# Twenty products of the identity's quarters on TensorE ahead of the first projection of a decoder layer

## What is computed

```python
x = _layernorm(x + _attn(x, x, x, sa_wq, ..., True), ln1_g, ln1_b)
x = _layernorm(x + _attn(x, encoder_output, encoder_output, ca_wq, ..., False), ln2_g, ln2_b)
x = _layernorm(x + _moe(x, router_w, router_b, e_w1, e_b1, e_w2, e_b2), ln3_g, ln3_b)
```

## Time and profile before

| | |
|---|---|
| median of 3 runs | 1040.5 us (1038.59 to 1041.3) |
| profiled execution, its own time | 1039.41 us |
| span of it, first to last instruction | 1037.7 us |
| TensorE busy | 977.9 us (94%) |
| DVE, ScalarE busy | 566.6 us, 585.7 us |
| GpSimd busy | 351.7 us |
| mean granted TensorE clock | 0.981 of 2.4 GHz |

### The profile page before, as it was taken

The page is one execution under the profiler, slowest core; times in us unless marked ns, Lnnn a source line. Parts: engine busy times, 40 slices in busy tenths (PEclk is TensorE's granted clock), DMA queues, the critical chain, the costliest instruction groups (busy, mean ns, idle before and its releaser), DMA issues.

```text
span 1037.7 us, 18756 instructions
## 1 busy us (share of the span) xinstructions
PE 977.9 (94%) x6068; PEld 583.6 (56%) x6069; DVE 566.6 (55%) x949; ACT 585.7 (56%) x1201; POOL 351.7 (34%) x481
## 2 busy tenths in 40 slices
PE   5899999999999999999998999988978999999975
PEld 3446444343445543445533354226977999999964
DVE  3646587777767777776777777804221221112127
ACT  2364556777765677765666757865323343443452
POOL 8465962343144443214445042122131111111114
PEclk9999999999999999999999999989998999999988
DMA  7623452003024012108114030022030343333143
GB/s 213 165 79 102 107 135 82 23 19 105 2 69 116 22 42 55 40 1 259 39 48 123 2 92 1 6 83 67 18 108 29 112 132 116 111 106 125 37 127 126
DMA packets 71936, 84.22 MB, mean 81 GB/s; under 512 B 10688, under 2 KB 65472, under 8 KB 71744
## 3 DMA queue, kind: packets, MB, share of 16 engines
q1 hardware_dynamic: 66368, 66.06, 22.2%
q0 software_dynamic: 5504, 17.34, 5.0%
HBM read 38.89 MB, written 12.63 MB: 50 GB/s over the span
## 4 chain that ended last, share of the span: by engine, by line
PE 86%; DMA 3%; SPq 3%; ACT 2%; issue 2%; DVE 2%; POOL 1%; another core or an unknown queue 1%; DVEq 0%; ACTq 0%; POOLq 0%
PE o_bank L798 16%; PE a_bank L781 15%; PE v_slot L1242 11%; PE v_slot L754 11%; PE a_bank L1234 9%; PE a_bank L722 6%; PE a_bank L737 3%; PE o_bank L1234 3%; PE v_slot L758 3%; PE v_slot L820 2%; SPq L498 2%; PE v_slot L806 1%; PE a_bank L702 1%; PE v_slot L759 1%
## 5 line engine op out<-in xcount | busy, mean ns | idle before, releaser
L969 DVE TENSOR_REDUCE max_q<-v_slot 128x1 f32<-128x1024 f32 (+3 forms) x352 | 399.6, 1172 | 115.0 <-PE v_slot L754 72.3
L912 ACT ACTIVATE probs<-a_bank 128x512 f32<-128x512 f32 (+1 forms) x688 | 364.2, 588 | 127.8 <-PE a_bank L781 115.9
L781 PE MATMUL a_bank<-q_stack_cross,k_stack_cross 99*128 99x512 bf16 x512 | 166.0, 386 | 7.3 <-issue 5.4
L1248 ACT ACTIVATE hidden<-a_bank,b 128x128 f32<-128x128 f32 x216 | 79.1, 368 | 163.6 <-PE a_bank L1234 141.5
L754 PE MATMUL v_slot<-k_stack_cross,q_stack_cross 96*128 96x512 bf16 x512 | 148.8, 383 | 2.5 <-DMA k_stack_cross<-parts 2.4
L798 PE MATMUL o_bank<-probs,v_cross 128*32 128x512 f32 x1024 | 133.3, 607 | 0.1
L1242 PE MATMUL v_slot<-stack_or_weights,hidden 128*128 128x256 f32 x576 | 131.0, 381 | 1.1 <-DVEq L1078 1.1
L1234 PE MATMUL a_bank<-x_col,stack_or_weights 128*128 128x128 f32 x864 | 112.6, 282 | 7.2 <-ACT hidden L1248 3.7
L1242 PEld LDWEIGHTS v_slot<-stack_or_weights,hidden 128*128 128x128 f32 x576 | 107.1, 191 | 14.7 <-DVEq L1078 1.3
L1234 PEld LDWEIGHTS a_bank<-x_col,stack_or_weights 128*128 128x128 f32 x864 | 108.5, 198 | 9.7 <-issue 4.1
L781 PEld LDWEIGHTS a_bank<-q_stack_cross,k_stack_cross 99*128 99x128 bf16 x512 | 44.9, 98 | 118.5 <-ACT probs L912 68.8
(11 more groups left out here) (210 smaller groups left out, 1162.0 us busy)
## 6 DMA issues: line engine op xcount, KB each, us to landing
stack_or_weights<-in_e_w SPq DMA_DIRECT2D x16, 1024.0 KB, 6.5
stack_or_weights<-parts SPq DMA_DIRECT2D x96, 128.0 KB, 2.4
k_stack_cross<-parts SPq DMA_DIRECT2D x96, 128.0 KB, 2.5
q_stack_cross<-parts SPq DMA_DIRECT2D x48, 128.0 KB, 2.4
inputs<-in_ctxT POOLq DMA_DIRECT2D x4, 1024.0 KB, 6.7
y_got<-token_out SPq DMA_DIRECT2D x16, 256.0 KB, 6.1
x_slots<-slots_in SPq DMA_DIRECT2D x30, 129.0 KB
inputs<-in_xT POOLq DMA_DIRECT2D x4, 512.0 KB, 6.0
```

The lines of the kernel that those rows point to most:

```text
L781: last = nc.tensor.matmul(bank[:, i * cols:(i + 1) * cols], lhs, q_stack[kind][0:KM, G * u + j, q0:S], start=True, stop=True)
L912: nc.scalar.activation(probs[tile % PB][:, js[0]:js[-1] + 1, q0:S], a_bank[at % AS][:, 0:len(js) * (S - q0)].rearrange("p (j t) -> p j t", ...
L969: nc.vector.tensor_reduce(most, rows, X, ALU.max, negate=True).then_inc(v_free, 1)
L1248: nc.scalar.activation(hidden[:, f, :], h_bank[f % HB][:, 0:P], ACT.Gelu, bias=b1[:, bass.ds(e * FC + f, 1)]).then_inc(flow.gelu_done, 1)
```

## The change

TensorE gets a prologue, `warm_up`. It waits until the identity is made and then forms products of a quarter of it (32 of its rows as the stationary operand, the same 32 rows repeated four times as 512 moving columns) in float32. Quarter g uses the partitions 32g to 32g+31, writes the bank g of `a_bank[0]`, `a_bank[1]`, `a_bank[2]`, `o_bank`, and nothing reads it: the first real product into each bank starts it anew. There are seven rounds with 4, 4, 2, 2, 2, 3 and 3 products. TensorE waits at the end of each until its last product is done, and the first `split` comes behind the seventh.

```diff
@@ -302,6 +302,7 @@
         passed = sem("passed")
+        products_done = sem("products_done")
@@ -681,7 +682,26 @@
+        def warm_up(pe):
+
+            pe.wait_ge(const_made, 8)
+
+            def quarter(g, bank):
+                rows = slice(32 * g, 32 * g + 32)
+                moving = ident[rows, :].rearrange("p (o c) -> p o c", o=1).to_broadcast([32, 4, P])
+                return nc.tensor.matmul(bank[:, 0:4 * P].rearrange("p (o c) -> p o c", o=4), ident[rows, :], moving, start=True, stop=True)
+
+            banks = [a_bank[0], a_bank[1], a_bank[2], o_bank]
+            rounds = 0
+            for tiles in (4, 4, 2, 2, 2, 3, 3):
+                for g in range(tiles):
+                    last = quarter(g, banks[g])
+                last.then_inc(products_done, 1)
+                rounds += 1
+                pe.wait_ge(products_done, rounds)
+
         def attention_tensor(pe):
+            warm_up(pe)
             pe.wait_ge(first_in, 32)
```

## The result

The changed kernel takes 1056.28 us (median of 4 runs, 1048.38 to 1060.82) against 1040.76 us (4 runs, 1038.59 to 1041.3): a ratio of 1.0146, 95% interval 1.0117 to 1.0175, slower by 1.5%. Timed again in the study, it took 1050.85 us against 1039.0 us, a ratio of 1.0125 (1.0103 to 1.0147). The forecast was slower by 5.0 us; the two measurements, as differences of medians, are 15.5 and 11.9 us. A ratio is worked out from all runs of its group, so that it can lie up to 0.2% beside the quotient of two medians. One run of the kernel before and one of `one_round` took over 1430 us (1434.62 and 1437.36 us), at a mean granted clock of 0.652 and 0.650, and no median or ratio here has them.

What follows compares the result with a forecast made beforehand. SyncE's issuing behind ScalarE's first copy was taken as the bound up to 42 us; a prologue ending at 15.86 us moves that copy from 12.83 to 17.82 us, so 1040.5 + 5.0 = 1045.5 us, range 1041.5 to 1051.8 us.

Steps and rivals of the forecast that it cites:

- What bounds the start: Up to 42 us SyncE's issuing, 24 transfers in 15.56 us, starts behind ScalarE's first copy without slack.
- the cover of the prologue: TensorE's idle time from 5.41 us until the first split at 9.04 us, 3.63 us in which the prologue costs nothing.
- The ceiling of the gain: ScalarE's first copy moves at best from 12.83 to 12.16 us, held by the biases: 0.67 us.
- The round's price: A prologue round of two, three or four products costs 2.14 us at 1.2 GHz or 1.16 us at 2.4 GHz.
- the rival without sharing: In the prologue, quarters do not share the array: shift +10.7 us, 1051.2 us, or +16 us, 1056.7 us; chance 0.09.
- I take 5.1 us: TensorE's clock rises after 5.1 us of prologue, 2.4 rounds, with 3.2 and 6.8 us as bounds.
- all steps behind it move along: Everything behind ScalarE's first copy shifts by the same +5.0 us, the scores from 42.2 to 47.2 us.
- the forecast's case: Products side by side, clock up in the prologue: first copy at 17.82 us, shift +5.0 us; chance 0.62.
- the clock does not rise in the prologue: Seven rounds and the first split run at 1.2 GHz: shift +11.4 us, 1051.9 us; chance 0.13.
- The range: For the whole kernel's time, the range holding 8 in 10: 1041.5 to 1051.8 us.

Runs made afterwards that it cites:

- one_round: The change cut to its first round of four quarter products; 1038.52 us, ratio 0.9993 to the kernel before.
- two_streamed: In place of the change's rounds, two products of the whole identity without any wait; 1039.38 us, ratio 1.0002 to the kernel before.
- full_rows: The change with one product of the whole identity (128 rows) in each of seven waited rounds; 1046.9 us, ratio 1.0084 to the kernel before.
- fours: The change with four quarter products in each of its seven waited rounds; 1050.39 us, ratio 1.0103 to the kernel before.
- same_no_pause: The change's own 20 products in the same order, with only one wait at the end; 1037.47 us, ratio 1.0070 to the kernel before.
- idle_delay: The kernel before without products, TensorE waiting for GpSimd to write a block of constants a second time; 1049.38 us, ratio 1.0116.
- twos_no_pause: The change with seven groups of two quarter products, waiting only behind the last; 1048.33 us, ratio 1.0097 to the kernel before.
- rows_96_stream: The change with seven one-piece products of 96 identity rows, without waits between them; 1034.04 us (one run).
- rows_96: The change with one one-piece product of 96 identity rows in each of seven waited rounds; 1052.73 us (one run).
- threes: The change with three quarter products in each of its seven waited rounds; 1054.93 us, ratio 1.0158 to the kernel before.
- rows_64: The change with one one-piece product of 64 identity rows in each of seven waited rounds; 1050.41 us (one run).
- the change, again: The unaltered change profiled and timed a second time; 1050.85 us, ratio 1.0125 to the kernel before.

## Why the prediction was wrong

Its sign was right and its size was not: 5.0 us forecast, 15.5 and 11.9 us measured, outside of the range.

- **What bounds the start** was right. The whole shift of the first copy, 11.51 us, arrives at the first scores (11.50 us); SyncE's 24 issues take 15.74 us as against 15.56 us. The one profile of before had `xt` land late, so that the cover of the prologue usually ends up to 1 us earlier than the 9.04 us I took.
- **The ceiling of the gain** was right in kind: it gave 0.67 us, and no time was won by `two_streamed`. The ceiling itself moves with the landings: in that profile the biases held ScalarE only until 10.83 us, not 12.16 us.
- **The round's price** was right: 2.14 us at half clock forecast, 2.18 and 2.14 us measured, 1.16 us at full clock against 1.18 us (`full_rows`) and 1.23 us (`fours`). Rounds of two, three and four take 2.14, 2.16 and 2.18 us, so the quarters share the array, and the rival without sharing is out. A round of four takes 1.02 of a round with one product of the whole identity, 2.18 against 2.13 us.
- **The step that failed** is "I take 5.1 us" for the rise of the clock. The 5.1 us came from an unbroken stream of full 128-row products, and I applied it to rounds with pauses, five of them with half or three quarters of the rows. With full rows it was nearly right: `fours` rose 6.0 us behind its first product and had its first copy at 18.60 us, against my 17.82 us. The change's rounds did not raise it at all: seven rounds ran at half clock where I had counted 2.4 of them, and the first split did, too, together 11.5 us.
- **A second step was too small**: "all steps behind it move along", that is, nothing is added behind the start. `fours` is the forecast's case, with the clock up in the prologue and the first copy at +5.8 us, and it still cost 1.03% (0.72 to 1.34%), 7.5 to 13.9 us. `full_rows`, at +5.75 us, cost 0.84% (5.8 to 11.5 us), and `same_no_pause`, at +3.4 us, 0.70% (5.0 to 9.4 us). Up to 1 us of this is the late landing in the profile of before; for the rest the profiles show the wait and the stretches at 0.50 above, and the cause stays open. `idle_delay` has no such surplus: +11.35 us at the copy, 1.16% (9.9 to 14.2 us).
- **The rival** "the clock does not rise in the prologue" gave +11.4 us and 1051.9 us and is what happened, to 0.1 us at the first copy of the first profile; the repeat's 1050.85 us lies beside it, the first median's 1056.28 us 4 us above. It had 0.13. The experiments bear out both its reasons in these kernels: without the waits the change's products rose after 5.0 us (`same_no_pause`), and with all 128 rows in each round they rose after 6.0 us (`fours`). I set against them only that the first split's stream had raised the clock, which is no evidence about rounds of another kind.
- **The range** ended at 1051.8 us, just where this rival began, and had no room for a scatter of several us behind the start, which the runs of the change showed (1048.38 to 1060.82 us).

## What to carry to other kernels

Before costing work meant to raise TensorE's clock, find in the trace a stretch of the same kind, in rows of the array used and in pauses, not only in time; here streams of 128 rows rose after 5.1 to 5.5 us, which said nothing about the stream of 64 that did not rise in 12.3 us. The prologue stood ahead of the first split in TensorE's order and cost its whole length beyond its cover: it ended at 20.5 us, 11.5 us behind the cover's 9.04 us, and the first copy came 11.5 us later. So size such a prologue at the clock it starts with; and ask first what the faster start could be worth, since here the next wait left 0.67 us and nothing of it was seen in the time. The first steps are one chain here, and a delay of the start went through to the end: 11.35 us of it cost 1.16%, about 12 us. The single profile of the kernel before had a load land after 7.5 us, the thirteen others after 6.2 to 7.3 us; take such a start from more than one.

## What the hardware showed that was not expected

A TensorE that is busy in the records stayed at half clock for 12.3 us without a pause in `twos_no_pause`. At the start of these kernels, with products of 512 float32 columns, the clock rose

- after 5.1 to 5.5 us of a stream of 128 rows (before, `two_streamed`, `idle_delay`),
- after about 6 us of rounds of 128 rows with 0.4 us of pause in 2.13 us (`full_rows`, `fours`),
- after 7.0 us of a stream of 96 rows (`rows_96_stream`), and 7.0 us after the start of a round of four quarters with 0.8 us of pause and the first split behind it (`one_round`);

it did not rise in 15 us of such rounds with 96 or 64 rows (`rows_96`, `threes`, `rows_64`), nor in 12.3 us of a stream with 64 (`twos_no_pause`). Behind a prologue that had not raised it, it rose 1.7 us (the change, again) to 5.2 us (`twos_no_pause`) into the first real products, by 2 us differently in two executions of one kernel (3.7 and 1.7 us). With rounds of 128 rows it rose at 11.5 us with one product (`full_rows`) and at 11.4 us with four row tiles (`fours`), and such a round took 2.13 us and 2.18 us.
